# A macaron block (FFN, mixing, FFN) on one core: the slots of phases 1 and 14 rewritten, a subtraction folded into weights, sigmoids written to PSUM

## The reference

```
x  = u
x1 = x  + 0.5 * FFN(layernorm(x))
x2 = x1 + MIX(layernorm(x1))
y  = x2 + 0.5 * FFN(layernorm(x2))

MIX(v):  xf = [v[0],  v[1:] @ WB.T ]          # along the 512 rows
         xb = [v[1:] @ WBf.T,  v[-1] ]
         gamma = sigmoid(xf @ w1.T + xb @ w2.T + b)
         return gamma * (xf + xb) + (1 - gamma) * v

FFN(v):  shared = silu(v @ Ws_up) @ Ws_down
         aff = v @ centroids.T                 # 64 experts
         top 8 experts by aff + bias; their weights are sigmoid(aff) over its sum
         every expert e: silu(v @ W_up[e]) @ W_down[e], times its weight, summed
```

## Time and profile before

| | us |
|---|---|
| median of 3 runs | 815.22 (815.02 to 815.83) |
| the profiled execution, its own time | 815.31 |
| its span | 813.5 |
| PE busy | 801.3 (99%) |
| DVE busy | 651.9 (80%) |
| ACT busy | 653.4 (80%) |
| POOL busy | 424.0 (52%) |

### The profile page before, as it was taken

How to read it: one execution, slowest core, us unless ns; L and a number is a source line. 1 busy time by engine, 2 the same in 40 slices (tenths; PEclk the granted TensorE clock), 3 DMA queues, 4 the chain that set the end, 5 groups by cost and what they waited for, 6 DMA issues and landing times.

```text
span 813.5 us, 12451 instructions
## 1 busy us (share of the span) xinstructions
PE 801.3 (99%) x3686; PEld 651.1 (80%) x3686; DVE 651.9 (80%) x1418; ACT 653.4 (80%) x1204; POOL 424.0 (52%) x377
## 2 busy tenths in 40 slices
PE   8999999999999999999999999999999999999998
PEld 5777878888888888888888888888888888888786
DVE  6987979879797787977879779797887878688775
ACT  6897779778887797968888688887878778786875
POOL 3885536454455554544545355464554545354453
PEclk9999999999999999999999999999999999999999
DMA  7000000000000000000000000000000000000000
GB/s 264 27 1 13 14 1 1 0 14 14 14 1 0 26 0 13 0 0 26 0 13 0 0 26 0 13 0 0 26 0 0 0 1 27 0 1 1 14 0 14
DMA packets 16046, 11.51 MB, mean 14 GB/s; under 512 B 1680, under 2 KB 14992, under 8 KB 16016
## 3 DMA queue, kind: packets, MB, share of 16 engines
q1 hardware_dynamic: 16016, 11.15, 4.4%
HBM read 9.05 MB, written 2.10 MB: 14 GB/s over the span
## 4 chain that ended last, share of the span: by engine, by line
PE 91%; ACT 3%; DVE 2%; POOL 2%; DMA 1%; SPq 1%; issue 0%; DVEq 0%
PE up L712 14%; PE up L713 14%; PE up L714 14%; PE y_ps L712 14%; PE y_ps L714 14%; PE y_ps L713 14%; PE side L721 3%; PE side L731 2%; POOL g_lo L358 1%; ACT up L430 1%; PE side L752 1%; PE side L751 1%; ACT g_hi L438 1%; ACT L430 1%; DMA wd_raw<-in_w_down 1%; DVE gated L584 0%
## 5 line engine op out<-in xcount | busy, mean ns | idle before, releaser
L358 POOL TENSOR_TENSOR g_lo<-gated,g_hi 128x512 fp32r<-128x512 f32 x256 | 334.1, 1305 | 347.4 <-ACT g_hi L438 346.7
L430 ACT ACTIVATE up<-up 128x512 f32<-128x512 f32 x528 | 310.1, 588 | 96.6 <-PE up L714 94.6
L584 DVE TENSOR_TENSOR gated<-up,cw 128x512 f32<-128x512 f32 x256 | 175.6, 686 | 86.6 <-ACT up L430 79.3
L712 PE MATMUL y_ps<-g_hi,wd_hi 128*128 128x512 f32 x512 | 207.7, 406 | 1.5 <-POOL g_lo L358 1.5
L712 PE MATMUL up<-x_hi,wu_hi 128*128 128x512 f32 x512 | 203.0, 396 | 0.4 <-POOL wu_lo L365 0.3
L713 PE MATMUL up<-x_lo,wu_hi 128*128 128x512 f32 x512 | 202.4, 395 | 0.0
L714 PE MATMUL y_ps<-g_hi,wd_lo 128*128 128x512 f32 x512 | 202.2, 395 | 0.0
L714 PE MATMUL up<-x_hi,wu_lo 128*128 128x512 f32 x512 | 202.0, 394 | 0.0
L713 PE MATMUL y_ps<-g_lo,wd_hi 128*128 128x512 f32 x512 | 201.6, 394 | 0.0
L584 DVE TENSOR_TENSOR up<-up,cw 128x512 f32<-128x512 f32 x256 | 176.8, 691 | 15.5 <-ACT up L430 11.7
L438 ACT CAST g_hi<-up 128x512 fp32r<-128x512 f32 x272 | 160.8, 591 | 29.8 <-DVE up L584 27.5
(11 more groups left out here) (102 smaller groups left out, 521.4 us busy)
## 6 DMA issues: line engine op xcount, KB each, us to landing
x_in<-in_x SPq DMA_DIRECT2D x8, 256.0 KB, 2.8
wu_raw<-in_w_up SPq DMA_DIRECT2D x4, 512.0 KB, 5.8
wd_raw<-in_w_down SPq DMA_DIRECT2D x4, 512.0 KB, 6.6
x_res<-in_x SPq DMA_DIRECT2D x8, 256.0 KB, 2.8
out<-out_sb SPq DMA_DIRECT2D x7, 256.0 KB, 2.2
out<-out_sb SPq DMA_DIRECT2D x2, 128.0 KB, 2.2
sm_raw<-in_ident SPq DMA_DIRECT2D x2, 64.0 KB, 5.1
ident<-in_ident SPq DMA_DIRECT2D x1, 64.0 KB, 2.4
```

Source lines behind the costliest of these rows:

```text
L358: nc.gpsimd.tensor_tensor(g_lo[:, i, :], gated[:, t // 2 % ORING, :], g_hi[:, i, :].bitcast(fp32), ALU.subtract).then_inc(lo_done[1], 1)
L430: nc.scalar.activation(up[i][:, :], up[i][:, :], ACT.Silu).then_inc(silu_done, 1)
L584: nc.vector.tensor_tensor(gated[:, t // 2 % ORING, :] if t % 2 else up[i][:, :], up[i][:, :], cw[ph.q][:, :], ALU.mult).then_inc(gate_done, 1)
L712: nc.tensor.matmul(o, a[0], b[0], start=start, stop=False)
```

## The change

- `AT_SECOND` and `AT_MID_PREP` (phases 1 and 14): every step of the mixing chain moves to earlier slots, the routing chain too, and `cw_t` and `cw_copy` go into slot 34 of the phase itself; phases 2 and 15 lose `late`. Fresh-chunk layernorm of phase 1 moves from slots 11 to 16 to slots 27 to 34.
- `AT_FIRST` (phase 0): `norm0` wholly in slot 11, `x_t` from slot 15 to 17, `sig` from 21 to 22, `inv` 28 to 29, `cw_t` 33 to 34, and POOL's low part of x two slots behind its high part (`x_low`, 31).
- `AT_THIRD`, `AT_STEADY_B`: `cw_t` from slot 19 to 22, `attn`, `tanh`, `gamma` from 25 to 26.
- The mix's `t1` is gone from every phase. Instead POOL once subtracts the identity from WB.T (`mix_weights`), and the weights for the first row are zeros instead of the identity, with one DMA less.
- The sigmoids go to PSUM, into free columns of the bank that holds `aff`; PE's `u_t` then waits for `gate` instead of `sig`.
- In DVE's slot order `x1` now stands ahead of the layernorm and routing steps of the same slot. POOL's split of the small weights at the start waits for the first layernorm.

```diff
 AT_FIRST = {
-    "x_t": 15, "x_copy": 15, "x_split": 29, "aff": 18, "sig": 21, "bias": 19, "max": 21, "take": 21,
-    "gate": 21, "sum": 21, "inv": 28, "cw_t": 33, "cw_copy": 33,
-    "stat0": (7, 8), "aggr0": 8, "rstd0": 9, "norm0": (11, 12),
+    "x_t": 17, "x_copy": 17, "x_split": 29, "x_low": 31, "aff": 20, "sig": 22, "bias": 20, "max": 22, "take": 22,
+    "gate": 22, "sum": 22, "inv": 29, "cw_t": 34, "cw_copy": 34,
+    "stat0": (7, 8), "aggr0": 8, "rstd0": 9, "norm0": (11, 11),
...
 AT_SECOND = {
-    "x_t": 27, "x_copy": 27, "x_split": 28, "aff": 29, "sig": 30, "bias": 29, "max": 30, "take": 30,
-    "gate": 30, "sum": 30, "inv": 34,
-    "y_t": 5, "x1": 6, "stat1": (7, 7), "aggr1": 8, "rstd1": 8, "norm1": (9, 10), "xu": 11, "u_t": 14,
-    "u_copy": 14, "attn": 17, "tanh": 18, "gamma": 16, "t1": 18, "x2": (19, 19),
-    "stat2": (20, 21), "aggr2": 21, "rstd2": 22, "norm2": (23, 23),
-    "y": 2,
-    "stat0": (11, 12), "aggr0": 13, "rstd0": 13, "norm0": (15, 16),
+    "y_t": 5, "x1": 4, "stat1": (4, 5), "aggr1": 5, "rstd1": 6, "norm1": (7, 8), "xu": 9, "u_t": 11,
+    "u_copy": 11, "attn": 13, "tanh": 13, "gamma": 14, "x2": (14, 14),
+    "stat2": (15, 16), "aggr2": 16, "rstd2": 17, "norm2": (18, 18),
+    "x_t": 21, "x_copy": 21, "x_split": 23, "aff": 24, "sig": 25, "bias": 23, "max": 25, "take": 25,
+    "gate": 25, "sum": 25, "inv": 31, "cw_t": 34, "cw_copy": 34,
+    "y": 2, "mix": 2,
+    "stat0": (27, 28), "aggr0": 29, "rstd0": 30, "norm0": (33, 34),
     "keep": 26,
 }
...
 AT_LAST = {
-    "y_t": 4,
-    "out": 4, "keep": 11, "late": 2,
+    "y": 2, "y_t": 5, "out": 5, "keep": 11,
 }
...
+            def mix_weights():
+                pool.wait_ge(small_in[0], 48)
+                pool.wait_ge(small_in[3], 48)
+                nc.gpsimd.tensor_tensor(sm_raw[:, A1:A1 + D], sm_raw[:, A1:A1 + D], ident[:, :], ALU.subtract).then_inc(mix_done, 1)
...
+            pool.wait_ge(norm_done[0], 1)
             nc.gpsimd.tensor_tensor(sm_lo[:, :], sm_raw[:, 0:A1], sm_hi[:, :].bitcast(fp32), ALU.subtract).then_inc(sm_lo_done, 1)
...
-                nc.scalar.activation(sig[:, :, :], aff, ACT.Sigmoid).then_inc(sig_done[q], 1)
+                nc.scalar.activation(sig, aff, ACT.Sigmoid).then_inc(sig_done[q], 1)
...
-                    if ph.at.get("t1") == t:
-                        dve.wait_ge(tanh_done, ph.mid + 1)
-                        nc.vector.tensor_tensor(att[:, :, 0:D], att[:, :, 0:D], normed[1][:, :, :],
-                                                ALU.subtract).then_inc(t1_done, 1)
```

More of the change, by code:

```diff
@@ L81 @@
     "x_t": 4, "x_copy": 4, "x_split": 5, "aff": 7, "sig": 9, "bias": 8, "max": 9, "take": 9,
-    "gate": 9, "sum": 9, "inv": 15, "cw_t": 19, "cw_copy": 19,
+    "gate": 9, "sum": 9, "inv": 15, "cw_t": 22, "cw_copy": 22,
     "y_t": 6, "x1": 8, "stat1": (10, 12), "aggr1": 13, "rstd1": 14, "norm1": (16, 18), "xu": 19, "u_t": 22,
-    "u_copy": 22, "attn": 25, "tanh": 25, "gamma": 25, "t1": 25, "x2": (27, 28),
+    "u_copy": 22, "attn": 26, "tanh": 26, "gamma": 26, "x2": (27, 28),
     "stat2": (29, 30), "aggr2": 30, "rstd2": 31, "norm2": (33, 34),
-    "late": 3,
+    "y": 2,
 }
@@ L96 @@
     "x_t": 1, "x_copy": 1, "x_split": 3, "aff": 6, "sig": 8, "bias": 7, "max": 8, "take": 8,
-    "gate": 8, "sum": 8, "inv": 15, "cw_t": 19, "cw_copy": 19,
+    "gate": 8, "sum": 8, "inv": 15, "cw_t": 22, "cw_copy": 22,
     "y_t": 6, "x1": 8, "stat1": (10, 12), "aggr1": 13, "rstd1": 14, "norm1": (16, 18), "xu": 19, "u_t": 22,
-    "u_copy": 22, "attn": 25, "tanh": 25, "gamma": 25, "t1": 25, "x2": (27, 28),
+    "u_copy": 22, "attn": 26, "tanh": 26, "gamma": 26, "x2": (27, 28),
     "stat2": (29, 30), "aggr2": 30, "rstd2": 31, "norm2": (33, 34),
@@ L187, in build @@
         zeros_r = sb("zeros_r", [P, P], fp32r)
-        sig, biased, taken = sb("sig", [P, NB, E]), sb("biased", [P, NB, E]), sb("taken", [P, NB, E])
+        biased, taken = sb("biased", [P, NB, E]), sb("taken", [P, NB, E])
         top = sb("top", [P, NB, TOPK])
@@ L200, in build @@
         att = side[:, :].rearrange("p (n c) -> p n c", c=AS)
-        aff = side1.rearrange("p (n d) -> p n d", n=NB)[:, :, 0:E]
+        aff, sig = (side1.rearrange("p (n d) -> p n d", n=NB)[:, :, k * E:(k + 1) * E] for k in range(2))
         side_rows = [s.rearrange("p (n d) -> p n d", n=NB) for s in (side0, side1)]
@@ L230, in build @@
         x1_done, xu_done, u_turned, u_copied = (sem(s) for s in ("x1_done", "xu_done", "u_turned", "u_copied"))
-        att_done, tanh_done, gamma_done, t1_done = (sem(s) for s in ("att_done", "tanh_done", "gamma_done", "t1_done"))
+        att_done, tanh_done, gamma_done, mix_done = (sem(s) for s in ("att_done", "tanh_done", "gamma_done", "mix_done"))
         x2_done, kept_done, out_done = sem("x2_done"), sem("kept_done"), sem("out_done")
@@ L316, in _ @@
             sp.dma_start(sm_raw[:, A2:A2 + D], wbf_t).then_inc(small_in[3], 16)
-            sp.dma_start(sm_raw[:, I1:I1 + D], ident_in).then_inc(small_in[3], 16)
             sp.dma_start(sm_raw[:, I2:I2 + D], ident_in).then_inc(small_in[3], 16)
@@ L345, in rstd_of, with x_high, x_low @@
                 nc.gpsimd.tensor_tensor(rstd[k][:, :], var_eps[k][:, :], neg_half[:, :], ALU.pow).then_inc(rstd_done[k], 1)
-            def x_split(q, n):
+            def x_high(q, n):
                 hold(pool, x_copied[q], n + 1)
                 nc.gpsimd.tensor_copy(x_hi[q][:, :], x_raw[:, :]).then_inc(x_hi_done[q], 1)
+            def x_low(q, n):
                 pool.wait_ge(x_hi_done[q], n + 1)
@@ L378, in phase @@
                         low_part(ph, t - 1)
+                    if ph.at.get("mix") == t:
+                        mix_weights()
                     if t in ph.at.get("wu_lo", ()):
@@ L399, in phase @@
                     if ph.at.get("x_split") == t:
-                        x_split(1 - ph.q, ph.prep[0])
+                        x_high(1 - ph.q, ph.prep[0])
+                    if ph.at.get("x_low", ph.at.get("x_split")) == t:
+                        x_low(1 - ph.q, ph.prep[0])
             nc.gpsimd.memset(neg_half[:, :], -0.5).then_inc(power_set, 1)
@@ L564, in select @@
                 dve.wait_ge(taken_done[q], n + 1)
-                nc.vector.scalar_tensor_tensor(w_sel[:, :, 0:E], taken[:, :, :], TAKEN, sig[:, :, :],
+                nc.vector.scalar_tensor_tensor(w_sel[:, :, 0:E], taken[:, :, :], TAKEN, sig,
                                                ALU.is_equal, ALU.mult).then_inc(sel_done[q], 1)
@@ L628, in phase @@
                         nc.vector.tensor_copy(sm_raw[:, A2 + D:A2 + AW], side0[:, 258:260]).then_inc(v_copied, 1)
+                    if ph.at.get("x1") == t:
+                        dve.wait_ge(y_turned, ph.p)
+                        dve.wait_ge(x_res_done, 16 * (ph.mid + 1))
+                        nc.vector.scalar_tensor_tensor(x1[:, :, :], side_rows[0], 0.5, x_res[:, :, :],
+                                                       ALU.mult, ALU.add).then_inc(x1_done, 1)
                     for k, c in ((0, ph.norm0), (1, ph.mid), (2, ph.mid)):
@@ L641, in phase @@
                             step(q, n)
[L642 to L646, removed]
-                    if ph.at.get("t1") == t:
-                        dve.wait_ge(tanh_done, ph.mid + 1)
-                        nc.vector.tensor_tensor(att[:, :, 0:D], att[:, :, 0:D], normed[1][:, :, :],
-                                                ALU.subtract).then_inc(t1_done, 1)
                     blocks, last = halves(ph, "x2", t)
                     if blocks:
-                        dve.wait_ge(t1_done, ph.mid + 1)
                         dve.wait_ge(gamma_done, ph.mid + 1)
@@ L665, in phase @@
                         last_sum(ph.p, ph.post)
-            nc.vector.memset(sm_raw[:, I1 + D:I1 + AW], 0.0)
+            nc.vector.memset(sm_raw[:, I1:I1 + AW], 0.0)
             nc.vector.memset(sm_raw[:, I2 + D:I2 + AW], 0.0)
@@ L747, in attention @@
                 pe.wait_ge(u_copied, c + 1)
+                pe.wait_ge(mix_done, 1)
                 for m in range(NB):
@@ L801, in phase @@
                     if ph.first and t == NJ:
-                        pe.wait_ge(small_in[3], 64)
+                        pe.wait_ge(small_in[3], 48)
                     if t == 0:
@@ L836, in phase @@
                         if ph.steady_b:
-                            pe.wait_ge(sig_done[q], ph.prep[0] + 1)
+                            pe.wait_ge(sel_done[q], ph.prep[0] + 1)
                         pe.wait_ge(norm_done[1], ph.mid + 1)
```

## The result

| | before | after |
|---|---|---|
| median of the runs | 815.3 (5 runs) | 819.45 (5 runs, 818.8 to 819.76) |
| ratio, 95% interval | | 1.005 [1.0035, 1.0064] |
| span of the profiled execution | 813.5 | 817.6 |

The account below looks back on a forecast made before the run. The prediction took PE's queue as the bound, PE being busy for 801.3 of 813.5 us. From the median 815.2 it took gains of 4.1 and added costs of 8.5 for 819.6, stated as 819.4, range 812.0 to 821.3.

Parts of the forecast that it names:

- PE's queue alone decides, steady phases don't move: Whole kernel: something counts only if PE waits or has an instruction less; steady even phases stay at 50.74 us.
- `u_t`: 1.5 in each phase: Slot 11 of phases 1 and 14: PE waits 1.5 us for the norms, 0.4 if they ran free of POOL.
- `x_t`: 1.1: Slot 21 of phases 1 and 14: PE waits 1.1 us for norms, `gamma` standing behind POOL's low part; between 0.1 and 1.7.
- `cw_t`: 1.8 and 1.0: Slot 34: PE waits for the routing weights, 1.8 us in phase 1 and 1.0 in phase 14.
- Restarts 0.5: After each of six new waits in phases 1 and 14 PE loses 0.08 us more, 0.5 together.
- Sum of the costs 8.5: Phases 1 and 14: waits at `u_t`, `x_t` and `cw_t` with their restarts, 8.5 us together.
- Sum of the gains 4.1: Old waits gone: phases 1 and 2 up to 1.88 us, phases 14 and 15 1.56, phase 0 0.7; together 4.1.
- Phase 0: POOL's wait at the end goes, 0.6 us; the `x_t` wait moves to slot 17, 0.1; gain 0.7, between 0.3 and 1.9.
- The sum of 819.6 lowered to 819.4: Whole kernel: 819.6 us taken as 819.4, because waits in a row help the late engine catch up.
- ACT takes 588 ns for silu into PSUM and 612 into SBUF: Sigmoids moved to PSUM on ACT: no difference that PE sees, so no cost.
- Rival 1: Phases 1 and 14: all three steps arrive in time and only the gains stay, 811.1 us; chance 0.2.
- Rival 2: Collisions of POOL and DVE fall otherwise, or later waits shrink: half the waits, 815.3 us, from 814 to 817; chance 0.2.

Follow-up runs that it names:

- old_chain: The changed kernel with the slot tables of phases 1, 2, 14 and 15 from the kernel before, all other edits kept; 815.39 us.
- mix_slot_later: The changed kernel with `u_t` and `u_copy` in slot 12 instead of 11, `attn` and `tanh` in 14 instead of 13, in phases 1 and 14; 816.54 us.
- chain_mended: The changed kernel, phases 1 and 14: `u_t` in slot 12, `attn` and `tanh` 14, `inv` 29; in phase 1 `stat0` and `aggr0` 13; 812.1 us.
- wd_hi_23: The changed kernel with ACT's seventh high part of w_down in slot 23 instead of 22 of phase 0; 819.26 us.
- wd_lo_14: The changed kernel with POOL's fourth low part of w_down in slot 14 instead of 13 of phase 0; 818.48 us.
- inv_29_stat0_13: The kernel of `inv_29` with the fresh chunk's statistics of phase 1 in slot 13 instead of 27 to 29; 816.54 us.
- gamma_13: The changed kernel with `gamma` in POOL's slot 13 instead of 14 in phases 1 and 14; 817.6 us.
- inv_29: The changed kernel with reciprocal and spread of the routing weights in slot 29 instead of 31 in phases 1 and 14; 818.41 us.
- norm0_split: The changed kernel with `norm0` of phase 0 in slots 11 and 12 instead of wholly in 11; 817.67 us.
- all_mended_wd_lo_14: The kernel of `all_mended` with POOL's fourth low part of w_down in slot 14 of phase 0; 810.91 us.
- all_mended: The kernel of `chain_mended` with, in phase 0, `norm0` in slots 11 and 12 and the seventh high part of w_down in 23; 810.98 us.

## Why the prediction was right

- *PE's queue alone decides, steady phases don't move.* Right: `old_chain` has DVE's load down from 651.9 to 645.8 us as well and equals the kernel before.
- *`u_t`: 1.5 in each phase.* Lost: 1.43 and 1.48. `mix_slot_later` and `chain_mended` take it away. The forecast took the collision with POOL as certain, and 0.4 for the wait without it. It fell so in both phases of the changed kernel's trace, but not always: in `wd_hi_23`, `wd_lo_14` and `inv_29_stat0_13` the list has 0.55 to 0.58 for phase 14, a loss of some 0.7. That the profiled execution has the full wait twice is in part luck, worth 0.8.
- *`x_t`: 1.1.* Lost: 0.95 and 0.95, and `gamma_13` shows its cause, the low part ahead of `gamma`. The replay gave `x2` to the last norm 7.9; it took 742.43 + 1.87 - 736.63 = 7.7. The four norms took 1.87 where they had taken 2.23.
- *`cw_t`: 1.8 and 1.0.* Lost: 1.68 and 0.92. Phase 5's rows, shifted by twelve slots, gave it, and `inv_29` and `inv_29_stat0_13` take it away.
- *Restarts 0.5.* 0.36. The 0.08 was read at an up product; at a turn of four transposes it is 0.06.
- *Sum of the costs 8.5:* measured 7.4 + 0.4 = 7.8. The term that is most off is `x_t`, 0.3 over both phases.
- *Sum of the gains 4.1:* measured 7.8 - 4.0 (spans, 817.57 - 813.53) = 3.8, but two terms of it were off in opposite directions. **Phase 0 was mis-sized**: 0.7 forecast, -0.1 measured. Its step on `x_t` held (the wait went to slot 17 at 1.48, forecast 1.5), and so did the one on POOL at its end. What I had not put in the sum is the wait of 0.75 in slot 27: with the sigmoid moved from slot 21 to 22 an ACT split of 0.62 came to stand ahead of it. `wd_hi_23` shows that this makes that wait, and also that taking it away gives back little. Another 0.25 is at the start: PE's first product with the experts' weights began at 11.62 instead of 11.37, behind a load that landed later. That is not the change's doing, since runs with the same code there have it at 11.37 (`wd_hi_23`) and 12.07 (`inv_29`). Phase 15, on the other side, shrank by 0.8 instead of 0.44. `old_chain`, with the tables of before, has 0.3 of it too, 53.4 instead of 53.7: at the very end the last stores took 1.8 instead of 2.2 us to land.
- *The sum of 819.6 lowered to 819.4, "since waits in a row help the late engine catch up":* no run shows that. The costs were forecast 0.7 too high and the gains 0.3, so that 819.4 met 819.45 within 0.1 is luck; the six waits, in their places and within 0.15 of their sizes, are not. The stated range of the costs, 5.3 to 9.3, also doesn't follow from the bounds of the terms, which add up to 3.3 and 10.0.
- *"ACT takes 588 ns for silu into PSUM and 612 into SBUF":* the row of 612 is not silu but the high part, which also reads from SBUF. The step on it held all the same: the sigmoid of phase 0 takes 0.37 into PSUM and took 0.38 into SBUF.
- *Rival 1, the chain holds, 811.1:* did not occur, but `chain_mended` at 812.1 shows that its price was right but for the 0.8 of phase 0. It needed other numbers in six table entries (`u_t`, `attn`, `tanh`, `inv`, `stat0`, `aggr0`), not a faster engine.
- *Rival 2, collisions fall otherwise, or later waits shrink when PE stops at an earlier one:* the first happened at one place in some executions, worth 0.8, not the 4 that the rival has. The second did not: each edit that removed a wait of phases 1 or 14 left the later ones at their size (`x_t` is 0.79 behind a `u_t` of 1.31 and behind one of 0.55).

What stays open: whether the faster executions of `norm0_split`, 0.8 beyond what its trace shows in phase 0, are those with the short wait at `u_t`.

## What to carry to other kernels

When one engine is the bound and work for it is prepared by others in a written-out order, average slack of those others says nothing: replay the stretch, instruction by instruction, from the rows of a similar stretch, and count what stands ahead of each step in its own queue. The cheap repairs are in that order: put a small step that unlocks others ahead of a long one on its engine, put side work where its engine idles anyway, and move a consumer by a slot before shortening anything. Here 6 us less work on an engine that is not waited for bought nothing.

## What the runs showed of the hardware

The same code at the same distance to POOL's instruction can be blocked or not. `norm1` of phase 14 in the changed kernel, and in `wd_hi_23` whose phase 14 is the same code (timelines of DVE and POOL):

```profile
723.88 1.71 DVE L549 TENSOR_SCALAR normed<-x,mv,rstd 128x128 f32<-128x128 f32 x2
...
724.22 1.29 POOL L359 TENSOR_TENSOR g_lo<-gated,g_hi 128x512 fp32r<-128x512 f32 x1 [0.37 <-ACT g_hi L451]
```

```profile
723.35 0.60 DVE L549 TENSOR_SCALAR normed<-x,mv,rstd 128x128 f32<-128x128 f32 x2
...
723.69 1.41 POOL L359 TENSOR_TENSOR g_lo<-gated,g_hi 128x512 fp32r<-128x512 f32 x1 [0.37 <-ACT g_hi L451]
```

POOL starts 0.34 after the first norm in both. Once the second norm is held up by POOL's whole instruction (1.71 for two), once it goes first (0.60) and POOL is the one that takes longer (1.41). PE's wait at `u_t` is 1.31 and 0.55 accordingly. Seven traced kernels have this code up to there, the changed one among them: the norms were blocked in all seven in phase 1, and in phase 14 in four. So one execution of an unchanged phase can differ by 0.8 us; with it single edits of that size are hard to tell.

The spread, a `tensor_tensor` of DVE with both inputs in SBUF, took 1.60 in `inv_29`, where POOL's low part had started 0.24 ahead of it. Where it started 0.19 ahead of POOL, in `inv_29_stat0_13`, it took 0.69, and POOL's instruction 1.66 instead of 1.29. So between these two it counts which starts first. Behind the start of POOL's `rstd`, an instruction of four columns, the spread keeps its 0.69 (at 115.65 in the changed kernel, `rstd` from 115.03 to 116.07). The Trainium skill, SBUF — State Buffer, section "Who interferes with whom", states that `tensor_tensor` with both inputs in SBUF contends with GpSimd's reads though it has no two-port mode; the row of `inv_29` agrees, and I had applied the rule to norms alone.

In the profiled execution of `all_mended_wd_lo_14` the granted clock was 0.55 in the mean of one early stretch, so mostly at the lower level of 1.2 GHz, where `all_mended` has 1.00 (view of windows: busy us and count by engine, then granted clock, DMA share, GB/s):

```profile
11.50:15.30 3.80, 3.73 (x9) 2.94 (x10) 3.01 (x6) 3.51 (x6) 1.25 (x2) 0.55 1.05 361
```

PE had been busy for 2.36 of the 3.50 us before it, and for 2.42 in `all_mended`, where the clock stayed up; the two traces show no reason for the difference. It began half as many matmuls there as `all_mended` did in the same stretch, 9 against 18, and the span is 1.2 us longer.
